# One-hots of the tile numbers laid out tile by tile, made by 25 comparisons with an immediate

## The reference, cut to what matters

```python
edge_index = jnp.stack([src, dst])
x = _layernorm(x + _L0_gnn_ref(x, edge_index, edge_type_16, ...), axis=-1)
x = _layernorm(x + _L1_gnn_ref(x, ..., node_type_4, edge_type_8, src, dst), axis=-1)
x = _layernorm(x + _L2_gnn_ref(x, edge_index, ...), axis=-1)
x = _layernorm(x + _L3_gnn_ref(x, ..., src, dst, edge_type_8, edge_weight), axis=-1)
# in each layer: messages by edge, then segment_sum(messages, dst, num_segments=n)
```

## Time and profile before

| | us |
|---|---|
| median of 3 runs | 3477.73 (3476.02 to 3478.45) |
| profiled execution, its own time | 3477.75 |
| its span | 3475.9 |
| busy: PE / PEld / DVE | 2882.9 / 1831.2 / 2560.1 |
| busy: ACT / POOL | 1946.9 / 2183.1 |

### The profile page before, as it was taken

How to read it: one execution, slowest core, us unless ns; L and a number is a source line. 1 busy time by engine, 2 the same in 40 slices (tenths; PEclk the granted TensorE clock), 3 DMA queues, 4 the chain that set the end, 5 groups by cost and what they waited for, 6 DMA issues and landing times. The chain is left out here.

```text
span 3475.9 us, 60577 instructions
## 1 busy us (share of the span) xinstructions
PE 2882.9 (83%) x15683; PEld 1831.2 (53%) x15683; DVE 2560.1 (74%) x6632; ACT 1946.9 (56%) x6316; POOL 2183.1 (63%) x2289
## 2 busy tenths in 40 slices
PE   5799799999987995777777767799999897887885
PEld 4666455555565553555555534577777653333332
DVE  8899889999977554888888843799999874444444
ACT  0478655555531452777777832588888753333333
POOL 1777667777756533666666445777777314777774
PEclk9999889999998997999999889799999996556555
DMA  6334478888841878777767544877777444333334
GB/s 180 97 104 127 139 248 264 262 262 263 262 114 38 275 318 334 248 210 212 208 199 204 134 159 173 233 227 225 229 226 226 130 182 170 102 103 103 103 103 104
DMA packets 260813, 651.81 MB, mean 188 GB/s; under 512 B 66813, under 2 KB 115658, under 8 KB 253706
## 3 DMA queue, kind: packets, MB, share of 16 engines
q0 software_dynamic: 141840, 474.50, 45.6%
q1 hardware_dynamic: 118650, 173.44, 15.6%
HBM read 505.78 MB, written 145.27 MB: 187 GB/s over the span
## 5 line engine op out<-in xcount | busy, mean ns | idle before, releaser
L2114 POOL DMA_INDIRECT a_rows<-table,met x568 | 557.4, 981 | 261.7 <-issue 135.4
L3690 PE MATMUL ps<-rows_in,hot_w 128*128 128x256 f32 x832 | 446.3, 646 | 100.7 <-ACT hot_w L3652 60.8
L1330 POOL DMA_INDIRECT rows_in<-table,met x416 | 412.6, 992 | 148.3 <-issue 85.2
L3640 POOL DMA_INDIRECT rows_in<-table,met x416 | 405.8, 976 | 144.2 <-issue 117.7
L3715 DVE TENSOR_TENSOR xs<-xs,ps 128x256 f32 x416 | 175.1, 421 | 304.1 <-PE ps L3690 300.4
L3690 PEld LDWEIGHTS ps<-rows_in,hot_w 128*128 128x128 f32 x832 | 197.0, 291 | 350.0 <-ACT hot_w L3652 183.8
L3652 ACT ACTIVATE hot_w<-hot,met 128x128 f32<-128x128 f32 x416 | 166.7, 401 | 373.7 <-PE ps L3690 340.2
L2114 POOL DMA_INDIRECT xs<-table,met x264 | 260.5, 987 | 115.7 <-issue 62.0
L2590 PE MATMUL ps<-a_rows,a_hot 128*128 128x260 f32 x1136 | 317.3, 403 | 17.9 <-DVE acc L2596 12.1
L833 POOL DMA_INDIRECT records<-rec,rows x241 | 260.3, 1080 | 88.9 <-issue 72.5
L2596 DVE TENSOR_TENSOR acc<-acc,ps 128x520 f32 x416 | 287.1, 690 | 35.3 <-PE ps L2590 14.4
(11 more groups left out here) (487 smaller groups left out, 6466.7 us busy)
## 6 DMA issues: line engine op xcount, KB each, us to landing
a_hot_t<-one_hots SPq DMA_DIRECT2D x104, 256.0 KB, 4.9
table<-stage SPq DMA_DIRECT2D x25, 1024.0 KB, 3.9
rows_in<-table,met POOLq DMA_INDIRECT x832, 3.7
dst_row<-slot_rows SPq DMA_DIRECT2D x52, 256.0 KB, 5.1
one_hots<-hot_t SPq DMA_DIRECT2D x52, 256.0 KB
by_dst<-dst_rows SPq DMA_DIRECT2D x25, 512.0 KB, 5.7
by_dst<-lo_rows SPq DMA_DIRECT2D x24, 512.0 KB, 4.7
a_rows<-table,met POOLq DMA_INDIRECT x568, 3.8
```

The lines of the kernel that those rows point to most:

```text
L1330: e.indirect_dma_start(self.rows[:, n % self.RING, 0:2 * D], None, self.table, bass.IndirectOffsetOnAxis(ap=self.b.met[:, n, R_SRC:R_SRC + ...
L2114: e.indirect_dma_start(self.row(n, 0, self.width), None, self.table, bass.IndirectOffsetOnAxis(ap=b.met[:, n, self.word:self.word + 1], ax ...
L3640: e.indirect_dma_start(self.rows[:, n % self.RING, :], None, self.table, bass.IndirectOffsetOnAxis(ap=self.b.met[:, n, R_REL:R_REL + 1], a ...
L3690: e.matmul(b.ps[:, n % self.BANKS, 0:D], self.hot_w[:, n % GRP_H, :], self.rows[:, n % self.RING, :], start=True, stop=True).then_inc(self ...
```

## The change

`hi_hot` is laid out `[P, NT, RC]` in place of `[P, RC, NT]`, with each tile's run of 391 columns padded to 392 (RC + RC % 2). It is made by 25 tensor_scalar comparisons of `hi_b` with the immediate t, each written to the contiguous columns of tile t, in place of one tensor_tensor of 9775 elements. The iota and the cast that made the row of tile numbers go. Three readers follow the layout: L531, L657 (moving operand, now a column of the layout) and L692 (now a turned view). Nothing else is changed.

```diff
-        self.hi = sb("hi_hot", [P, RC, NT], BF16)
+        self.hi = sb("hi_hot", [P, NT, RC + RC % 2], BF16)
...
-        tile_i, tile_b = sb("tile_i", [P, NT], I32), sb("tile_b", [P, NT], BF16)
...
-            e.iota(tile_i[:, :], pattern=[[1, NT]], base=0, channel_multiplier=0)
...
-            e.tensor_copy(tile_b[:, :], tile_i[:, :])
...
-            e.tensor_tensor(r.hi[:, :, :], tile_b[:, :].unsqueeze(1).to_broadcast([P, RC, NT]),
-                            hi_b[:, :].unsqueeze(2).to_broadcast([P, RC, NT]), ALU.is_equal).then_inc(hot_made, 1)
+            for t in range(NT):
+                last = e.tensor_scalar(r.hi[:, t, 0:RC], hi_b[:, :], float(t), None, ALU.is_equal)
+            last.then_inc(hot_made, 1)
...
-                    last = e.matmul(ps[:, 4, k * NT:(k + 1) * NT], r.lo_hot[:, blk % 2, :, k], r.hi[:, c, :],
+                    last = e.matmul(ps[:, 4, k * NT:(k + 1) * NT], r.lo_hot[:, blk % 2, :, k], r.hi[:, :, c],
...
-                last = e.matmul(b.ps[:, 7, k * NT:(k + 1) * NT], r.lo_hot[:, blk % 2, :, k], r.hi[:, blk * BLK + k, :],
+                last = e.matmul(b.ps[:, 7, k * NT:(k + 1) * NT], r.lo_hot[:, blk % 2, :, k], r.hi[:, :, blk * BLK + k],
...
-            G, hi = self.looks(blk), r.hi[:, c0:c0 + n, :]
+            G, hi = self.looks(blk), r.hi[:, :, c0:c0 + n].rearrange("p t c -> p c t")
```

## The result

The changed kernel takes 3481.56 us (median of 20 runs, 3478.25 to 3486.18) against 3474.83 for the kernel before (20 runs, 3470.92 to 3478.45). The ratio is 1.002, with a 95% interval of 1.0014 to 1.0026: some 7 us slower, right at the edge of the 0.2% that count as no change. The forecast was 3478.8, the range 3471 to 3487.

A forecast was written before the change was run, and what follows sets the result against it. VectorE was taken to set the head, and VectorE and TensorE both to be full in ranking blocks 10 to 19. Forecast: 3477.75 - 5.8 (head) + 6.8 (ranking) = 3478.8 us, range 3471 to 3487.

The forecast's parts named there:

- Comparisons: In the head on VectorE: 25 comparisons at 0.18 us each replace 10.26 us, a gain of 5.8 us.
- Rival (d): In the head: comparisons don't run four at a time and take 0.48 us each, total 3486.3 us; 5%.
- Room on the sync queue: In the head: the sync queue is idle 15.5 us before the barrier, so no transfer limits the gain.
- Product: In the ranking, L692 on VectorE: reading hi_hot 784 bytes apart adds 0.25 us per call, 0.50 us per block.
- Rival (a): In the ranking: skipping reads are free at L692, so only the head counts, 3472.0 us; 15%.
- Rival (b): In the ranking at L692: the far stride costs VectorE more than 64 bytes, 0.50 us per call, 3487.0 us; 14%.
- Which blocks swallow it: In the ranking: block 0 pays 0.5 us; waits in blocks 1 and 2 and blocks 3 to 8 swallow theirs.
- Slack in the full blocks: In the ranking: VectorE's waits before block 21 absorb 0.9 us of 13 x 0.50, leaving row numbers 6.15 us later.
- idle time on TensorE: In the ranking: TensorE, full until now, would get about 0.4 us of idle time per block.
- The end of the ranking: The ranking grows by 6.8 us; block 24's slack of 3.2 us covers its own added time.
- TensorE's fetch: Matmuls L531 and L657: fetching moving columns 784 bytes apart hides behind the weight load and costs 0.
- rival (c): In the head: TensorE's fetch comes on top of the weight load, 105 ns a matmul, +10.4, 3489.2 us; 8%.

The follow-up runs named there:

- e6: Changed kernel, hi_hot read along the columns and the product written to SBUF 200 bytes apart, on the second chip: 3900.98 us, ratio 0.9991 to the kernel before.
- e3: Changed kernel with hi_hot laid out block by block, 32 bytes between tiles in place of 784: 3487.11 us, ratio 1.0035 to the kernel before.
- The fill: Fill of 450 fp32 columns on VectorE ahead of each block's products: in the kernel before 3486.43 us (1.0032), in the changed kernel 3493.46 us (1.0056).
- e1: Changed kernel with the product run columns innermost and written over its PSUM operand: 3470.62 us, ratio 0.9988 to the kernel before.
- e9: Changed kernel, hi_hot read along the columns and the product written to SBUF 200 bytes apart, on the third chip: 3476.27 us, ratio 1.0007 to the kernel before.

## Why the prediction was right, and where its steps were not

The case that was forecast is the one that came: the head gains, the products lose more, TensorE's fetch stays hidden in the head, and the time is within the range, 2.8 us above the forecast figure by the median and 2.3 by the profiled execution (3481.07). That closeness is in part luck. The forecast was a change of +1.0 us on a starting point of 3477.75, and the measured change is +6.7 by the medians, +3.3 by the profiled executions; the starting point was itself 2.9 above the median of 20 runs, which hides part of the miss.

- **Comparisons.** Forecast 0.18 us each, first `lo_hot` at about 11.0 and the barrier near 55.9. Measured 0.171, 10.66 and 55.8: a gain of 5.9 for 5.8. Rival (d) is gone. The support from L733 was weaker than the prediction has it: measured are 260 ns for 391 columns, so 416 at that rate would be some 267, and L733's 330 lies well above.
- **Room on the sync queue.** Forecast enough; 9.7 us are left.
- **Product.** Forecast +0.25, measured +0.295 (862 ns). This term was mis-sized. L807 against L796 had said 0.31; taking L493 because it reads was the wrong pick, since e6 shows that a read and a write make the instruction equally long. By the Trainium skill, "Vector Engine (DVE) Microarchitecture Reference", section Measured stream behaviour on trn2, a source that hops at every element takes 1.73 ns a column against 1.054. The page measured 4-byte words; an estimate from it would be 0.27 us for 400. The measurement of this kernel, with its 2-byte elements, is 0.295, a little above. Rival (a) is gone. Rival (b), that the far stride costs more, is refuted by e3.
- **Which blocks swallow it.** Block 0 paid 0.6 for a forecast of 0.5. Blocks 1 and 2 were to be free; the second paid 0.55. Blocks 3 to 8 swallowed theirs, as said. Up to block 9 this is 1.2 in place of 0.5.
- **Slack in the full blocks.** This step failed. I counted 0.9 us of waits as all the slack that VectorE had before block 21. Its own loop, though, can be read from after: 14.07 us a block, where it sets the period, less 0.59, is 13.48, against the 13.72 at which TensorE held it. The fill gives the same loop (14.07 - 0.59), and so does the skipping write (13.99, less the 1.57 - 1.05 of its pair, is 13.47). So VectorE had 0.24 us a block to spare, some 3 us in thirteen blocks, in gaps too short to be listed as waits. What an unhindered period adds is 14.07 - 13.72 = 0.35, not the 0.50 less 0.07 that I charged. That the forecast period, 14.1, came out is luck: the too small price and the too small slack nearly cancel.
- **The clock.** Not foreseen at all: two falls of TensorE's clock in blocks 9 to 20, worth 2.1 us. With them, and with the 0.4 of the first period, these blocks cost 6.3. Forecast was 0.4 us of idle time on TensorE a block; measured was 0.85 in all eleven.
- **The end of the ranking.** Forecast +6.8; measured +9.7 from the barrier to the last scatter (413.85, before 410.07): 1.2 up to block 9, 6.3 in blocks 9 to 20, 2.1 behind. The reading that block 24 adds nothing of its own and passes on the shift held: the last full block begins at 398.36, 3.8 later than before, and the last scatter is 3.8 later.
- **TensorE's fetch.** Forecast 0 in the head: right, 32 matmuls in 2.34 us as before, so rival (c) is gone. In the full blocks it costs 0.4 us (e1), where TensorE is the bound again. The argument that it is hidden behind the load doesn't explain why a matmul grew from 212 to 223 ns; its size is what made it harmless.

What stays open: the traces put the loss at 3.3 us and three medians at 6.7, 11.8 and 6.3. The decodings of three traces of the changed kernel (423.09, 423.39, 424.29) are 3.6 to 4.8 after that of the one trace of before. The medians scatter by more than this. The traced execution of e3, the longest, has some 5 us more than the others behind the decoding's start; whether that is where the changed kernel's longer executions lose time too is not shown.

## What to carry to other kernels

The price of a layout is paid at each of its readers, on the engine that reads: 10.3 us of one instruction became 4.4, and 49 products, each 0.295 us longer, took back more than that. Where two engines are nearly tied, find the loop of each by itself before charging one of them. And if one side has to skip, let it be the PSUM side: with the product turned and left in PSUM, the new comparisons are kept, the price goes, and the kernel is faster than both (3470.62 and 3469.95 us), if only by 0.12 and 0.14% against the one before.

## What the hardware did that I had not expected

- A bf16 comparison that writes 2-byte elements 50 bytes apart takes 1267 ns for 391 of them, against 260 when they are side by side; start to start 22.27/25 = 0.89 us against 0.171, five times. A skipping write of fp32, 200 bytes apart, costs only 0.295 us for 400. The Trainium skill, "Vector Engine (DVE) Microarchitecture Reference", section Measured stream behaviour on trn2, also has small steps dearer than large ones; no run here varies the step of one write alone.
- VectorE pays nothing for 200 bytes between elements in PSUM, on read and write at once (576 ns against 577), and nothing for 8 bytes between 4-byte words in SBUF (L796, 592 ns for 416 elements).
- In blocks 9 to 20 TensorE's clock falls to the level of 1.2 GHz, for 3 to 4 us each time, only in kernels whose TensorE has small gaps there: none in the kernel before and the two runs with the product in PSUM, which have none. The falls don't follow the idle time strictly: none with 0.6 us idle in eleven periods (e9), two with 0.85 (after) and with 1.4 (the changed kernel on the third chip), three with 2.2 (e3), four with 4.1 (the fill on top), but only one with 2.45 (the fill in the kernel before). Whether the gaps bring the falls about was not tried by itself.
- A moving operand of 25 columns, 784 or 32 bytes apart, makes a matmul 11 ns longer (212 to 223).
- One chip of the three of the experiments ran every kernel 12% slower, that of before too, with a granted clock in the ranking of about 0.9 (0.98 for the kernel before in the first 420 us of its trace). Its cause was not looked for.
